# In the expert loop, GpSimd issues the scatter of an expert's result first and the gather of a later expert behind it

## What is computed

```python
scores = softmax(xf @ gate_w.T)
_, idx = top_k(scores + gate_b, K)                  # E = 64 experts, K = 6
xb = zeros((E, CAP, D)).at[se, pos].set(xf[tok], mode='drop')   # CAP = 128, D = 256
h = silu(einsum('ecd,eid->eci', xb, w1)) * einsum('ecd,eid->eci', xb, w3)   # I = 176
yb = einsum('eci,edi->ecd', h, w2)
y = zeros_like(xf).at[tok].add(contrib * wf[:, None])
z = silu(xf @ ws1.T) * (xf @ ws3.T) @ ws2.T
return (y + z).reshape(shape)
```

## Time and profile before

| | us |
|---|---|
| median of 3 runs | 1903.85 |
| lowest and highest run | 1903.59, 1912.81 |
| the profiled execution's own time | 1909.18 |
| its span in the profile | 1907.3 |
| first expert stage, first to last scatter issue | 348.2 to 547.1 |
| second expert stage, first to last scatter issue | 1705.5 to 1903.2 |

### The profile page before, as it was taken

The page is one execution under the profiler, slowest core; times in us unless marked ns, Lnnn a source line. Parts: engine busy times, 40 slices in busy tenths (PEclk is TensorE's granted clock), DMA queues, the critical chain, the costliest instruction groups (busy, mean ns, idle before and its releaser), DMA issues. The chain is left out here.

```text
span 1907.3 us, 32059 instructions
## 1 busy us (share of the span) xinstructions
PE 1791.9 (94%) x10553; PEld 1102.0 (58%) x10554; DVE 1311.0 (69%) x3400; ACT 1124.8 (59%) x2292; POOL 843.5 (44%) x923
## 2 busy tenths in 40 slices
PE   6999999999957799999999999999799999989997
PEld 3666666777733355555555555555456666667776
DVE  4777776566638577777777777777277777756664
ACT  5777775125424667777777777777477777721111
POOL 1111101777746666566655555550011111147776
PEclk9999999999977899999999999999899999999999
DMA  2424341999933333333333333332222433249996
GB/s 77 128 84 142 95 131 56 264 258 258 260 77 94 95 100 103 101 102 101 102 101 102 101 101 102 90 90 58 66 86 73 129 108 123 80 143 261 263 259 145
DMA packets 192287, 243.72 MB, mean 128 GB/s; under 512 B 17559, under 2 KB 159607, under 8 KB 192126
## 3 DMA queue, kind: packets, MB, share of 16 engines
q1 hardware_dynamic: 166286, 202.62, 35.0%
q0 software_dynamic: 24576, 37.77, 10.3%
q10 hardware_dynamic: 1264, 1.31, 0.2%
HBM read 126.65 MB, written 63.86 MB: 100 GB/s over the span
## 5 line engine op out<-in xcount | busy, mean ns | idle before, releaser
L1403 DVE TENSOR_REDUCE a_smax<-a_p_ring 128x1 f32<-128x512 f32 (+2 forms) x768 | 355.2, 506 | 134.1 <-PE a_p_ring L1494 128.5
L1302 ACT ACTIVATE a_probs<-a_p_ring 128x512 f32<-128x512 f32 x640 | 368.2, 607 | 109.0 <-PE a_p_ring L1506 107.7
L1494 PE MATMUL a_p_ring<-p_ks,p_qs 100*128 100x512 bf16 (+3 forms) x1024 | 246.6, 307 | 16.3 <-ACT a_smaxT L1339 5.5
L1506 PE MATMUL a_p_ring<-p_qs,p_ks 103*128 103x512 bf16 (+3 forms) x1024 | 243.4, 304 | 6.7 <-ACT a_probs L1302 5.8
L50 POOL TENSOR_TENSOR f_rstd<-f_mv,eps 128x4 f32<-128x4 f32 x31 | 14.8, 478 | 497.8 <-DVE f_mv L44 495.5
L676 ACT ACTIVATE e_silu<-e_p_up 128x176 f32<-128x176 f32 x128 | 40.6, 318 | 313.0 <-PE e_p_up L768 313.0
L519 PE MATMUL f_p_up<-f_xnT,ws1T 128*128 128x512 f32 x384 | 187.4, 611 | 1.1 <-ACT f_xnT L300 1.1
L1522 PE MATMUL a_p_out<-a_probs,p_v 128*32 128x512 f32 (+3 forms) x2048 | 177.6, 448 | 6.1 <-ACT a_probs L1302 6.1
L561 PE MATMUL f_p_z<-ws2T,f_hidden 128*128 128x256 f32 (+1 forms) x768 | 180.6, 384 | 0.7 <-DVE f_hidden L397 0.7
L137 POOL DMA_INDIRECT h_got<-rows,slot_token x128 | 125.8, 983 | 123.9 <-DVE slot_token L496 83.0
L519 PE MATMUL f_p_up<-f_xnT,ws3T 128*128 128x512 f32 x384 | 180.5, 592 | 0.0
(11 more groups left out here) (171 smaller groups left out, 3613.8 us busy)
## 6 DMA issues: line engine op xcount, KB each, us to landing
h_w<-w_in SPq DMA_DIRECT2D x128, 352.0 KB
p_qs<-a_parts SPq DMA_DIRECT2D x192, 128.0 KB, 2.4
p_ks<-a_parts SPq DMA_DIRECT2D x192, 128.0 KB, 2.4
h_w<-w_in SPq DMA_DIRECT2D x128, 176.0 KB
rows<-first_row SPq DMA_DIRECT2D x16, 640.0 KB, 6.4
rows<-f_row SPq DMA_DIRECT2D x16, 640.0 KB, 6.6
x<-x_in SPq DMA_DIRECT2D x16, 512.0 KB, 5.7
acc<-x SPq DMA_DIRECT2D x16, 512.0 KB, 3.3
```

The source lines that it names most:

```text
L1302: nc.scalar.activation(to[:], p_score[s][:], ACT.Exp, scale=SCALE).then_inc(score_free[s], 1)
L1403: ins = nc.vector.tensor_reduce(smax[:, t, 4 * g + h:4 * g + h + 1], p_score[s][:, at:at + length], AX.X, ALU.max)
L1494: ins = nc.tensor.matmul(p_score[s][:, at:at + length], qs[1 - u][0:SR + MASK, 4 * g + h, t * P:(t + 1) * P], ks[1 - u][0:SR + MASK, 4 * g ...
L1506: ins = nc.tensor.matmul(p_score[s][:, at:at + length], ks[u][0:SR + MASK + TOP, 4 * g + h, t * P:(t + 1) * P], qs[u][0:SR + MASK + TOP, 4 ...
```

## The change

Within one step of GpSimd's loop, the gather of expert e + 12 now stands behind the scatter of expert e. The step waits for `y_scaled`, then for the scatter two before, issues the scatter, and then the gather. No transfer is added or removed, and no other engine's code is touched.

```diff
@@ -660,10 +660,10 @@
                     pool.wait_ge(to.acc_stored[u], 16 * B // XR)
                 for e in range(E):
                     pool.wait_ge(y_scaled, e + 1)
+                    wait_count(pool, added[e % 2], 16 * (e // 2))
+                    add(e)
                     if e + GATHERS < E:
                         gather_rows(nc, w, dram, to, e + GATHERS)
-                    wait_count(pool, added[e % 2], 16 * (e // 2))
-                    add(e)
                 for n in range(2):
                     pool.wait_ge(added[n], 16 * E // 2)
```

## The result

The changed kernel is slower: 1915.41 us (median of 16 runs) against 1904.99 us (median of 16 runs of the kernel before, the first three among them). The ratio is 1.005, 95% interval 1.0035 to 1.0064. The prediction was 1901.3 us with a range of 1898 to 1906; the time lies 10.4 us above before and outside the range. The profiled execution has a span of 1913.7 us, against 1907.3.

What follows compares the result with a forecast made beforehand. Both expert stages were taken to end GpSimd-bound, though TensorE is full. Two stages at 1.29 us each made 2.6 us less, with no other cost: 1903.85 - 2.6 = 1901.3 us, range 1898 to 1906.

Steps and rivals of the forecast that it cites:

- 3.18 us step: GpSimd's steady gather and scatter with their issue take 3.18 us, against 3.15 us per result from VectorE.
- the chain of landings: At each stage's end, scatters wait for the landing two before; four pairs took 17.93 us, 4.48 each.
- The lead of 1.29 us: Without its step's gather ahead, scatter 2 starts 1.29 us earlier, carried to scatter 50 and kept in each stage's tail.
- The late gather: Each moved gather stands 1.89 us later in GpSimd's queue; the last keeps 10.1 us of cover, so it costs nothing.
- The wait for the landing moves ahead of the gather: In GpSimd's queue the gather now follows this wait; equal-parity scatters stay 6.37 us apart, so the wait is no longer.
- The slower rival: Scatter landings grow past 6.07 us and delay GpSimd's queue; 0.1 us more per pair gives 1906 us; chance 0.11.
- Swallowed: GpSimd catches up or late landings take back the gain before stage end: 1903.85 us, or down to 1902.6; chance 0.30.
- more: GpSimd's landing waits, 4.9 us per stage, shrink too: 1896.3 us at the limit, 1899 likelier; chance 0.09.

## Why the prediction was wrong

**What bounds the kernel** was read rightly. GpSimd decides where both stages end though TensorE is full, by its 3.18 us step and the chain of landings. The kernel with both waits on the gather showed how hard that chain can bind.

**The lead of 1.29 us** was right at scatter 2, in both stages (0.28 us behind the result). Its worth at the end was not shown: the reordering with cheap waits came out at 1.0002, within an interval that holds 0.9986 and 1.

**The late gather costs nothing** held: TensorE's results take the same 195 to 197 us.

**The step that failed** is "The wait for the landing moves ahead of the gather", with "so the wait is as long as it was". The rows of the instruction lists stood in my own text: a scatter waited for `added` before, and for `added` and `y_scaled` after. I counted what the two events cost and nothing for having both in front of one transfer. It puts the landing wait on a separate instruction, 0.78 us from landing to scatter in place of 0.28. The size follows. A pair of scatters is 6.37 us apart, so a landing delays the queue above 6.37 - 0.28 = 6.09 us before, and above 6.37 - 0.78 = 5.59 now, with the median at 5.7 to 6.0 between the two. In the changed kernel's second stage, the one where the trace has the landings of both parities (scatters 1 to 48), 34 lie above 5.59 us and 17 above 6.09, by 22.9 and 9.6 us in sum. A delay of one parity delays the other too, so not all of it adds up. An estimate with the queue's step of 3.185 us and these 48 landings, each scatter starting at the later of its step and the landing two before plus the reaction, gives 14.4 us of waits at a reaction of 0.79 us and 7.6 at 0.27. The trace has 15.0, against 5.7 in the kernel before, which had its own landings.

**The slower rival** had the right place (the landing as the edge on which GpSimd's pace stands, median 6.0 against a threshold of 6.07) and the right price per 0.1 us, but the wrong mover. It let the landings grow, which they did not; the threshold came down by 0.5 us. With 0.11 I held it unlikely because nothing would move the landings, and did not ask what would move the threshold. The 6.07 itself was a slip in kind: I took 0.30 us of issue for the reaction, right for one wait only.

**Swallowed and more** did not happen. That the tail had this cost already I had passed over, though my rows showed it: 4.48 us per pair of scatters, where a landing took 3.8.

## What to carry to other kernels

When a DMA on GpSimd has two waits, write first in the code the wait whose event comes last. Here that alone, in the twelve last scatters of the kernel before, gave 0.25%, and the opposite cost 0.35 to 0.7%. When an edit moves instructions, compare the waits of each instruction as well as its place; and where a transfer's landing is close to the step of its queue, price every tenth of a us on either side.

## What was not expected of the hardware

GpSimd's start after an event comes 0.23 to 0.31 us later where the wait is the transfer's only one, or the one written first, and 0.72 to 0.84 us later in nearly all pairs where it is a second wait written last (a few pairs show 1.1 to 1.9 us, and why is open). The trace has the wait written last on an instruction of its own, and a third wait on that same instruction. Why that costs 0.5 us no run here shows. It is so for the landings of scatters, and for VectorE's result at the scatters of expert 2 with the waits in the other order (0.78 and 0.80 us). A wait that is already met leaves no mark on the queue: transfers with two waits still start 0.30 us behind the one before.
